# A fused embedding, attention and expert kernel on one core: keys scaled jointly, turns and products in another order around each pair of sequences

## What is computed

```python
h  = concat([cls, patches @ W + b + pos, txt])          # (8, 178, 192)
xn = layernorm(layernorm(h)) * ln_w
Q  = xn[:, None] * W_qk[None, :, None]                  # 12 heads, scaled copies of xn
A  = softmax(causal(Q @ Q.T / sqrt(192)))
O  = (A @ (xn - mean(wte, axis=0))) / (position + 1)    # wte: 50257 x 192
h  = h + concat_heads(O) @ W_o.T
h  = h + shared_expert(layernorm(h)) + top4_of_16_experts(layernorm(h))
```

## Time and profile before

| | |
|---|---|
| median of 3 runs | 482.19 us |
| the profiled execution's own time | 482.77 us |
| its span, first to last instruction | 481.0 us |
| PE busy | 456.2 us (95%) |
| DVE busy | 291.7 us (61%) |
| ACT busy | 175.4 us (36%) |
| POOL busy | 102.0 us (21%) |
| mean granted TensorE clock | 0.996 |
| share of the expert stage | about 285 to 481 us |

### The profile page before, as it was taken

The page is one execution under the profiler, slowest core; times in us unless marked ns, Lnnn a source line. Parts: engine busy times, 40 slices in busy tenths (PEclk is TensorE's granted clock), DMA queues, the critical chain, the costliest instruction groups (busy, mean ns, idle before and its releaser), DMA issues. The chain is left out here.

```text
span 481.0 us, 7316 instructions
## 1 busy us (share of the span) xinstructions
PE 456.2 (95%) x2656; PEld 392.5 (82%) x2656; DVE 291.7 (61%) x814; ACT 175.4 (36%) x573; POOL 102.0 (21%) x111
## 2 busy tenths in 40 slices
PE   3999989999899998999998999999999999999997
PEld 3577659966689665797666999998999999999996
DVE  7677876276761687726487716687546754654343
ACT  1366556045660546512435026442312222221211
POOL 6013111221112222110013104830170017100000
PEclk9999999999999999999899999999999999999999
DMA  8967999999999999977107022222232322222230
GB/s 208 243 242 149 211 214 214 212 214 214 213 213 214 213 214 213 212 141 219 67 1 271 1 64 61 63 60 65 72 63 63 77 71 63 61 78 73 71 67 25
DMA packets 23686, 65.00 MB, mean 135 GB/s; under 512 B 2876, under 2 KB 13332, under 8 KB 23266
## 3 DMA queue, kind: packets, MB, share of 16 engines
q0 software_dynamic: 7904, 40.86, 40.4%
q1 hardware_dynamic: 14882, 22.68, 17.7%
q10 hardware_dynamic: 864, 1.00, 0.8%
HBM read 61.88 MB, written 1.27 MB: 131 GB/s over the span
## 5 line engine op out<-in xcount | busy, mean ns | idle before, releaser
L512 ACT ACTIVATE pm<-bank,nmax 128x128 f32<-128x128 f32 x96 | 34.0, 366 | 106.2 <-DVE nmax L1003 106.2
L1092 DVE TENSOR_TENSOR area_b<-area_b,area_w 128x356 f32<-128x356 f32 x64 | 33.9, 529 | 62.4 <-ACT area_b L580 62.3
L788 PE MATMUL bank<-woT,area_o 128*128 128x192 f32 (+1 forms) x432 | 71.4, 327 | 0.0
L788 PEld LDWEIGHTS bank<-woT,area_o 128*128 128x128 f32 (+1 forms) x432 | 70.0, 182 | 0.4
L418 POOL DMA_DIRECT2D area_w<-in_L_attn_wte_dram x26 | 31.4, 1227 | 127.1 <-DMA area_w<-in_L_attn_wte_dram 127.1
L735 PE MATMUL bank<-pT,xn 128*128 128x356 f32 x96 | 38.8, 486 | 6.8 <-issue 5.2
L869 PE MATMUL bank<-area_w_r,area_o_r 128*128 128x356 f32 x112 | 43.9, 392 | 0.0
L580 ACT ACTIVATE area_b<-bank,area_k 128x356 f32<-128x356 f32 x32 | 17.9, 559 | 58.9 <-PE bank L873 58.9
L905 PE MATMUL bank<-area_k,area_b 128*128 128x192 f32 (+1 forms) x192 | 36.8, 327 | 0.0
L870 PE MATMUL bank<-area_w_r,area_o_r 128*128 128x356 f32 x112 | 36.4, 325 | 0.0
L538 ACT ACTIVATE area_b<-xb,w 64x192 f32<-64x192 f32 x96 | 34.4, 454 | 0.0
(11 more groups left out here) (216 smaller groups left out, 1002.1 us busy)
## 6 DMA issues: line engine op xcount, KB each, us to landing
area_w<-in_L_attn_wte_dram POOLq DMA_DIRECT2D x28, 1344.0 KB, 12.7
area_w<-gate_rows SPq DMA_DIRECT2D x64, 178.0 KB, 3.0
area_k<-in_experts_dram SPq DMA_DIRECT2D x8, 353.0 KB, 5.8
area_a<-in_experts_dram SPq DMA_DIRECT2D x6, 353.0 KB, 6.4
woT<-in_L_attn_W_o_dram SPq DMA_DIRECT2D x1, 1728.0 KB, 16.1
area_o<-in_x_dram SPq DMA_DIRECT2D x4, 384.0 KB, 9.6
area_w<-area_w POOLq DMA_DIRECT2D x1, 1344.0 KB, 10.8
area_b<-in_experts_dram SPq DMA_DIRECT2D x3, 353.0 KB, 8.1
```

The lines of the kernel that those rows point to most:

```text
L512: last = act.activation(pm[:, sl, j, :], bank[0][:, j * P:(j + 1) * P], ACT.Exp, bias=nmax[:, sl, j:j + 1], accum_out=psums[:, sl, j:j + 1])
L788: last = pe.matmul(o, oT[:, c, at:at + n], woT[:, c, :], start=(c == 0), stop=(c == NCH - 1))
L1092: dve.tensor_tensor(sil[:, n % 2, :], sil[:, n % 2, :], wbc[:, m % RING, :], ALU.mult).then_inc(weighted, 1)
```

## The change

Seven edits:

1. DVE makes the scaled keys of a group of four heads with one `tensor_tensor` on 128x768 instead of four `tensor_scalar` on 128x192.
2. PE's `turn_in(0)` of the next pair moves from behind `turn_probs(3)` to behind `turn_probs(4)`, right ahead of `mix(4)`; `turn_in(1)` moves behind `turn_probs(5)`. ACT's `turn_out` and `prob_out(5)` move along, and its `queries_b` of group 1 moves to the end of the pair.
3. DVE: `keep(0)` moves from u=4 to behind `mix_out(4)`; `queries` of group 0 moves behind `tails_out(4)`, groups 1 and 2 behind `mix_out(5)`.
4. DVE: `norm_end` of the next pair is split, one sequence at each of two units.
5. In the last pair `turn_a(0)` stands behind `turn_probs(4)`, `turn_b(0)` behind `turn_probs(5)`, and ACT's `features_b(0)` behind `prob_out(5)`.
6. At the start PE runs 6 products of zeros (128x192, float32) ahead of the wait for the patch weights, and 12 more behind `embed(0)`; they read `wrest`, which POOL has cleared, so POOL's load into `wrest`, and with it all its transfers behind it, also waits for the first scores. `embed(1)` moves behind the first scores, its `embeds_out(1)` behind the third `queries`.
7. At the start DVE takes the statistics of the two text tiles ahead of `embeds_out(0)`.

```diff
@@ -422,6 +422,7 @@
 
             rstd(4, 1)
             pool.wait_ge(s_wo, 16)
+            pool.wait_ge(scores_tail, 1)
             pool.dma_start(wrest[0:WREST, :], wte[P * WROWS:V, :]).then_inc(wte_rest, 16)
 
             add_rows(0)
@@ -589,7 +590,7 @@
                     if i == 0 and u < UPB:
                         act.wait_ge(xnT_ready, 4)
                         queries_b(1, 1, [u])
-                    if u == 3 and not last:
+                    if u == 4 and not last:
                         turn_out(0, 2 * i + 2)
                     if u == 3 and last:
                         w_high(0)
@@ -598,19 +599,19 @@
                         w_high(1)
                     if u == 4 and not last:
                         act.wait_ge(xnT_ready, 4 * i + 6)
-                        queries_b(0, 2 * i + 2, [0, 1])
+                        queries_b(0, 2 * i + 2, [0])
                 mix_out(4, U + 4)
+                prob_out(5, U + 5)
                 if last:
                     features_b(0)
                 if not last:
                     turn_out(1, 2 * i + 3)
-                prob_out(5, U + 5)
                 if not last:
                     exps(0, U + 6)
                 mix_out(5, U + 5)
                 if not last:
                     act.wait_ge(xnT_ready, 4 * i + 8)
-                    queries_b(0, 2 * i + 2, [2])
+                    queries_b(0, 2 * i + 2, [1, 2])
                     queries_b(1, 2 * i + 3, range(UPB))
 
             for i in range(PAIRS - 1):
@@ -650,9 +651,15 @@
                     last = pe.matmul(emb_bank[i][:, 0:E], ximg[:, i, k, :], wtok[:, k, :], start=(k == 0), stop=(k == KX - 1))
                 last.then_inc(s_embps, 1)
 
+            def keep_awake(count):
+                for _ in range(count):
+                    pe.matmul(bank[0][:, 0:E], wrest[:, 0:P], wrest[:], start=True, stop=True)
+
+            pe.wait_ge(pool_own, 4)
+            keep_awake(6)
             pe.wait_ge(s_tokw, 16)
             embed(0)
-            embed(1)
+            keep_awake(12)
             pe.wait_ge(s_const, 1)
 
             def turn_in(b, bt, i):
@@ -796,6 +803,7 @@
             pe.wait_ge(s_pad, 3)
             queries_in(0, 0)
             scores(0, 0)
+            embed(1)
 
             def mean():
 
@@ -833,18 +841,17 @@
                         mean()
                     if u == 2 and last:
                         mean_projected()
+                    turn_probs(u, U + u)
                     if u == 4 and last:
                         turn_a(0)
-                    turn_probs(u, U + u)
-                    if u == 3 and not last:
+                    if u == 4 and not last:
                         turn_in(0, 2 * i + 2, i + 1)
                 mix(4, U + 4, i)
+                turn_probs(5, U + 5)
                 if last:
                     turn_b(0)
                 if not last:
                     turn_in(1, 2 * i + 3, i + 1)
-                turn_probs(5, U + 5)
-                if not last:
                     queries_in(2 * i + 2, 0)
                     scores(0, U + 6)
                 mix(5, U + 5, i)
@@ -958,11 +965,12 @@
                     last = dve.tensor_tensor(hin[0:NPOS, 2 * i + half, 0, :], emb_bank[i][rows, 0:E], postab[rows, :], ALU.add)
                 last.then_inc(s_hin, 1)
 
-            def stats_begin(tiles, add):
+            def stats_begin(tiles, add, done=()):
 
                 n = len(tiles)
                 for t, src in enumerate(tiles):
-                    own.mark(dve.bn_stats(st[0:src.shape[0], t, :], src))
+                    if t not in done:
+                        own.mark(dve.bn_stats(st[0:src.shape[0], t, :], src))
                 dve.wait_ge(dve_own, own.at)
                 dve.memset(pause[:], 0.0)
                 for t, src in enumerate(tiles):
@@ -970,13 +978,13 @@
                 dve.wait_ge(dve_own, own.at)
                 dve.tensor_scalar(ve[:, 0:n], mv[:, 0:n, 1], add, None, ALU.add).then_inc(var_ready, 1)
 
-            def norm_begin(h):
-                stats_begin([h[:, 0, 0, :], h[:, 0, 1, :], h[:, 1, 0, :], h[:, 1, 1, :]], EPS * EPS / (1.0 + EPS))
-
-            def norm_end(i, h):
+            def norm_begin(h, done=()):
+                stats_begin([h[:, 0, 0, :], h[:, 0, 1, :], h[:, 1, 0, :], h[:, 1, 1, :]], EPS * EPS / (1.0 + EPS), done)
+
+            def norm_end(i, h, batches=range(2)):
 
                 dve.wait_ge(rstd_ready, i + 1)
-                for b in range(2):
+                for b in batches:
                     for t in range(2):
                         own.mark(dve.tensor_scalar(z[:, b, t, :], h[:, b, t, :], mv[:, 2 * b + t, 0:1],
                                                    rs[:, 2 * b + t:2 * b + t + 1], ALU.subtract, ALU.mult))
@@ -991,11 +999,11 @@
 
             def queries(b, bt, groups=range(UPB)):
                 dve.wait_ge(xnT_ready, 2 * bt + 2)
-                for h in range(GRP * groups[0], GRP * (groups[-1] + 1)):
-                    last = dve.tensor_scalar(qa[:, b, :, h, :], xa[:, b, :].rearrange("p (c t) -> p c t", c=3),
-                                             w2a[:, h:h + 1], None, ALU.mult)
-                    if h % GRP == GRP - 1:
-                        last.then_inc(qa_ready, 1)
+                for g in groups:
+                    heads = slice(GRP * g, GRP * g + GRP)
+                    keys = xa[:, b, :].rearrange("p (c a t) -> p c a t", c=3, a=1).broadcast_to([P, 3, GRP, 64])
+                    scales = w2a[:, heads].rearrange("p (c j t) -> p c j t", c=1, t=1).broadcast_to([P, 3, GRP, 64])
+                    dve.tensor_tensor(qa[:, b, :, heads, :], keys, scales, ALU.mult).then_inc(qa_ready, 1)
 
             def maxima(u, U):
                 sl = u % 2
@@ -1112,23 +1120,25 @@
                     src = bank[4][:, t * E:(t + 1) * E] if t < 2 else bank[5][0:n, 0:E]
                     dve.tensor_tensor(R[0:n, 3 * i + t, :], src, R[0:n, 3 * i + t, :], ALU.add).then_inc(out_read, 1)
 
+            dve.wait_ge(s_text[0], 48)
+            for t in (1, 3):
+                own.mark(dve.bn_stats(st[:, t, :], hin[:, t // 2, 1, :]))
             embeds_out(0)
-            dve.wait_ge(s_text[0], 48)
             dve.wait_ge(s_hin, 1)
-            norm_begin(hin[:, 0:2])
+            norm_begin(hin[:, 0:2], (1, 3))
             dve.wait_ge(s_small, 32)
             dve.scalar_tensor_tensor(out=w2[:], in0=w2[:], scalar=SCALE, in1=w2[:], op0=ALU.mult,
                                      op1=ALU.mult).then_inc(s_w2, 1)
             dve.wait_ge(s_w2, 1)
             link(dve.tensor_scalar(lnw[:], lnw[:], (1.0 + EPS) ** -0.5, None, ALU.mult))
             norm_end(0, hin[:, 0:2])
-            embeds_out(1)
             queries(0, 0, [0])
             keep(0, 0)
             keep(1, 0)
             queries(0, 0, [1])
             maxima(0, 0)
             queries(0, 0, [2])
+            embeds_out(1)
 
             def rows(v, n):
                 return v.rearrange("p (t a) -> p t a", a=1).broadcast_to([P, 3, n])
@@ -1199,10 +1209,9 @@
                         mix_out(u - 1, U + u - 1)
                     if i == 0 and u < 2:
                         embeds_out(2 + u)
+                    tails_out(u, U + u)
                     if u == 4 and not last:
-                        keep(0, i + 1)
                         queries(0, 2 * i + 2, [0])
-                    tails_out(u, U + u)
                     if i == 0 and u < UPB:
                         queries(1, 1, [u])
                     if i == 0 and u == 0:
@@ -1239,17 +1248,19 @@
                             correct(1)
                     if not last:
 
-                        if u == (2 if i == 0 else 1):
-                            norm_end(i + 1, hin[:, 2 * i + 2:2 * i + 4])
-                        if u == 4:
-                            queries(0, 2 * i + 2, [1, 2])
+                        at = u - (2 if i == 0 else 1)
+                        if at in (0, 1):
+                            norm_end(i + 1, hin[:, 2 * i + 2:2 * i + 4], [at])
                 divide(5, U + 5)
                 mix_out(4, U + 4)
+                if not last:
+                    keep(0, i + 1)
                 tails_out(5, U + 5)
                 if not last:
                     maxima(0, U + 6)
                 mix_out(5, U + 5)
                 if not last:
+                    queries(0, 2 * i + 2, [1, 2])
                     keep(1, i + 1)
                     queries(1, 2 * i + 3)
                     if norms:
```

## The result

| | before | after |
|---|---|---|
| median of the runs of this comparison | 482.05 us (4 runs) | 474.34 us (4 runs, 474.07 to 476.25) |
| ratio of after to before, 95% interval | | 0.9856 [0.9821, 0.9892] |
| the profiled execution | 482.77 us | 476.25 us |
| its span | 481.0 us | 474.4 us |
| PE busy | 95% | 459.4 us (97%) |

The change makes the kernel 7.7 us faster by the medians, 6.5 us by the two profiled executions. The second is the like for like: in both, the first scores run at the lower clock level and the clock falls once more in the last pair. The forecast was 476.4 for the median and 477.0 for the profiled execution.

The account below looks back on a forecast made before the run. PE, busy 95%, was taken as the bound. Start +0.9, boundaries -5.3, norm_end -0.3 and -0.7, last pair -0.4 sum to -5.8 us: from the median 482.19 to 476.4, range 473.8 to 478.6.

Parts of the forecast that it names:

- Boundaries, -5.3: At three pair ends, mix(4) starts 1.87 us behind its turns, turning z lying between: 1.76 us gained each.
- 0.3 us is spare: At a boundary, unit 5's probabilities are ready at T+4.3, PE wants them at T+4.6; T is turn_probs(4)'s start.
- the forecast's own sign of being wrong: Listed signs of error: DVE's unit 5 probabilities later than mix(4), or PE standing before L808 or the scores behind it.
- Joint keys: DVE's scaled keys: one instruction takes 0.94 us instead of 1.36 for four; 10 us of DVE saved, off PE's path.
- the rival at 1.9 us: Joint keys at their upper bound: PE waits 0.65 to 0.8 us per boundary, 478.5 us in all; chance 10%.
- norm_end, -0.3 and -0.7: Splitting norm_end removes PE's waits ahead of scores: 0.3 us in the first pair, 0.7 in the third.
- Last pair, -0.4: In the last pair, turn_a(0), 0.4 us, fills part of the 0.8 us wait behind unit 4's turns.
- Start, +0.9: At the start the clock falls again before the first scores, embed(1) lies on PE's path: unit 1 0.9 us later.
- the clock stays up: Rival at the start: the clock holds into the first scores, start -0.5 instead of +0.9, 475.0 us; chance 25%.
- The table: The table's fold and DVE's sum hold PE only if it comes over 5.9 us earlier; 5.4 was expected.
- POOL's added wait: At the start, POOL's wait for the first scores ends before W_o lands and costs 0.
- Turns in a row: Rival: 1.8 us of turns together, twice per boundary, lower the clock, 1.65 us each; six give 486.3 us; chance 4%.

Follow-up runs that it names:

- experiment 6: Changed kernel with norm_end of both sequences in one piece at one unit again; median 477.33 us, ratio 0.9903 to the kernel before.
- experiment 9: Kernel before with only the joint scaled keys and the split norm_end, old orders and start; median 477.31 us, ratio 0.9922.
- experiment 10: Changed kernel with the turns of z, turn_a and turn_b and ACT's copies back in their old places; median 478.44 us, ratio 0.9928.
- experiment 5: Changed kernel with a group's scaled keys made by four instructions again; median 476.16 us, ratio 0.9883 to the kernel before.
- experiment 3: Kernel before with only the zero products, late embed(1) and embeds_out(1), and POOL's wait; DVE's early statistics left out; median 480.87 us, ratio 0.9995.
- experiment 1: Changed kernel run again with no edit; median 475.47 us, ratio 0.9869 to the kernel before.
- experiment 11: experiment 7 with embed(1) ahead of the first turn again, embeds_out(1) back, and 8 zero products on each side of embed(1); median 474.42 us, ratio 0.9843.
- experiment 7: Changed kernel with 18 zero products instead of 12 behind embed(0), 2 more between the turns and 1 behind them; median 474.93 us, ratio 0.9845.
- experiment 2: Changed kernel with all start edits undone (zeros, late embed(1) and embeds_out(1), early statistics, POOL's wait); median 474.81 us, ratio 0.9854.
- experiment 8: Changed kernel with the mean's one-column products one unit later, behind the scores of unit 3; median 477.88 us, ratio 0.9909.

## Why the prediction was right

**Boundaries, -5.3.** Right in mechanism and size. Forecast: product 1.87 us behind the turns; measured 1.86. Gain per boundary 1.76; measured 1.85 in pair 2, where the norm's split changes nothing (experiment 6). The stages around the first boundary gave 1.27 + 0.98 = 2.25, which is 1.85 and the norm's 0.39 below; the first 0.87, the earlier turn of z taken away, lies ahead of unit 5. Which edit makes it was not split in the forecast; the runs split it into 0.42, 0.56 and 0.87 (experiments 9, 10).

"0.3 us is spare" for unit 5's probabilities holds at the first two boundaries: they are ready at 64.42 + 0.69 = 65.11, and PE turns them at 65.48, right behind the mix. It does not hold at the third, where PE waits 0.28 for them. DVE has one more product there, ahead of the division:

```profile
185.93 0.75 DVE L1226 TENSOR_TENSOR wbar<-wbar,woT 128x576 f32<-128x576 f32 x1
```

It is one of the two rows from which the price of a joint key was taken, but in the forecast's chain for this boundary it is missing. It costs 61.22 - 60.86 = 0.36 us. So the forecast's own sign of being wrong, DVE's probabilities later than `mix(4)`, came true once in three times. The spare is what joint keys buy: with single keys 0.1 is lost in pair 2 and 0.4 in pair 3 (experiment 5).

**Joint keys.** 0.94 us forecast, 0.952 measured. The Trainium skill (VectorE: DVE Perf Modes, The perf-mode tier table) puts float32 `tensor_tensor` in the slower mode; an estimate by that alone made 2.7 us of the 1.36 of four in a row. The trace does not bear that out as the price of the exchange, in which one instruction stands for four. Which part of the 0.41 us saved is the fixed part, no run separates. The repeated inputs cost nothing that shows, and the rival at 1.9 us is out.

**norm_end, -0.3 and -0.7.** Right place, and right size in the old order: split there, it gives 0.39 us in pair 1 (experiment 9). In pair 3 the two waits of before, this one of 0.55 and the one of 0.36 for unit 5's probabilities, together cost 63.92 - 62.71 = 1.21, so this one some 0.85 at most; the other is missing in the forecast. In the changed kernel the whole norm_end would hold PE for longer (0.62 and 0.87, where before it was 0.32 and 0.55), and the split is worth 0.78 and 1.10 (experiment 6): the rest is gain of the other edits that a whole norm_end would take back. Pair 3 as a whole gave 63.92 - 61.22 = 2.70 against a forecast of 2.46. It is 1.85 + 1.21 - 0.36: the forecast lacked the wait for unit 5's probabilities in both kernels, 0.36 each, and by luck they cancel.

**Last pair, -0.4.** 35.91 - 35.53 = 0.38, with the fall in both executions; 34.21 - 33.91 = 0.30 without it (experiments 3 and 1).

**Start, +0.9.** Right in the reason (the clock falls between the zeros and the first scores: 2.05 us, and `embed(1)` lies on the path), half the size: 26.50 - 26.08 = +0.42. The first scores began 1.0 us earlier and not 0.6, since the two groups of turns, which begin at the upper level, also follow each other faster (16.96 - 15.33 = 1.63 against 2.03). The number is that of two executions, and partly luck: with this start unit 1 began at 25.92 to 26.62 in seven profiles, and with the old one at 24.73, 25.14 and 26.08. What failed outright is a bound: POOL's row gives W_o's landing as 25.56 "at the latest", which was true as said, but I used it as the time that gates, and with the clock up put unit 1 at 25.6. POOL's row goes from 23.85 to 25.56 between kernels for the same load, and PE's own wait in experiment 11 ends at 23.59. So the rival "the clock stays up" was undersized: 2.7 us in the trace, not 1.4.

**The table.** Right that it does not hold PE: sum at 222.2, mean at 223.41. But its lead did not move as I reasoned. Piece 2 was issued at 37.17 (forecast 37.7) and SP's row came at 219.84, not 221.5. Where piece 2 is issued earlier the fold comes earlier: issued at 34.35, 34.42 and 35.88 (experiments 11, 7, 2), SP's row is at 217.19, 217.88 and 219.02, and in all profiles 182.7 to 184.4 us lie between the two. An earlier start pulls the table along, and it became the bound in none. One term at nothing was wrong: POOL's added wait for the first scores was to end before W_o lands, but POOL's row in the changed kernel, at 25.35, is released by the first scores (PE, L700); it moved piece 2 by nothing that shows (37.23 before). I had named DVE's wait for the fold, but not that its 2.0 us are hidden by the mean alone (experiment 8):

```profile
219.85 1.56 DVE L1235 TENSOR_TENSOR area_w<-area_w 128x1344 f32<-128x1344 f32 x1 [2.00 <-DMA area_w<-area_w]
```

**Turns in a row and the clock** (the rival that ended slower). No boundary of any kernel has a granted clock under 1, so it is out: 1.8 us of turns between products did not lower it here.

**The sum.** Terms measured, at +0.42, boundaries and norm together up to the mean -6.80 and the last pair -0.38, give -6.76, against -5.8. The span differs by 6.6. The profiled execution took 476.25 (forecast 477.0). The median is 1.9 us lower still, because three of the four runs had, by their mean clock, no fall in the last pair; the forecast had priced that branch at 1.65 and put it in the range only. So the median fell within the range with two misses on the same side, terms 1.0 us too small and the missing fall; its lower end, 473.8, was 0.5 us away.

## What to carry to other kernels

When an engine waits behind a step for two other engines' copies, put there the work that is independent of them and exactly as long; and on the copying engine put the copy ahead of the next stage's preparation. Before adding work to hold the clock, look at the idle stretch right ahead of the products it is meant for: zeros that end 2.8 us ahead of the first turn bought nothing; six more there, two between the turns and one behind them brought unit 1 2.7 us forward. When a step comes round several times, list what its engines do at each: the third boundary had a product that the first two had not. And a small wait of the old schedule can grow in the new one (0.32 to 0.62, 0.55 to 0.87).

## What the runs showed that I had not expected

- The same binary falls into groups 1.9 us apart by one clock fall (experiment 1), so a comparison of medians also compares in how many executions the clock fell. Best (experiment 11) is 2.8 us shorter than the changed kernel where both fell (spans 471.6 and 474.4), and its stages from unit 1 on are the same, yet the medians are alike (474.42, 474.34): all six of its runs are at a mean clock of 0.996, the value of a start without and a last pair with a fall. By the mean clock, the fall came in five of six runs in experiment 7 and in four of ten of the changed kernel. Whether a faster start makes the later fall likelier, the runs do not settle; one run of 471.9 shows what both together give.
- The fall comes at or just behind 15 products of a single column, 2.4 us with PE busy at 1.00 throughout, in eight of the thirteen profiles without wide products between them. With nine of 192 columns between and behind them it was gone from the profile. A kernel with fewer or narrower ones wasn't tried, and would have to cost under 1.7 us.
- W_o is the same load in every kernel, and POOL waits for it from about 14 us on; where its wait is put down to W_o it ends anywhere from 23.85 us (best) to 25.56. Why, no run tells.
